# The scores of a graph layer computed only where the two triangles need them, and every engine's order written anew

## What is computed

```python
adj_tri = jnp.triu(adj, k=1)
diag_mask = jnp.triu(adj, k=0) - adj_tri
for l in range(L):
    m_left = jnp.einsum('bsh,oh->bso', h, W_left[l])
    m_right = jnp.einsum('bsh,oh->bso', h, W_right[l])
    u_left = jnp.einsum('bih,bjh->bij', h, m_left) / temper
    u_right = jnp.einsum('bih,bjh->bij', h, m_right) / temper
    u = u_left * adj_tri + u_left * diag_mask + u_right * jnp.swapaxes(adj_tri, 1, 2)
    delta_exp_u = jnp.exp(u) * adj
    attention = delta_exp_u / (jnp.sum(delta_exp_u, axis=2, keepdims=True) + 1e-10)
    h_lin = jnp.einsum('bsh,oh->bso', h, W_lin[l]) + b_lin[l]
    h = jax.nn.relu(_layer_norm(jnp.matmul(attention, h_lin), ln_a[l], ln_b[l]))
```

## Time and profile before

| | us |
|---|---|
| median of three runs (2846.2 to 2848.68) | 2846.78 |
| the profiled execution, device time | 2846.03 |
| its span, first to last instruction | 2844.2 |
| PE busy in it | 2792.3 (98%) |
| DVE busy | 2447.5 (86%) |
| ACT busy | 1784.8 (63%) |
| POOL busy | 1497.1 (53%) |
| mean granted TensorE clock | 0.992 |

### The profile page before, as it was taken

The page is one execution under the profiler, slowest core; times in us unless marked ns, Lnnn a source line. Parts: engine busy times, 40 slices in busy tenths (PEclk is TensorE's granted clock), DMA queues, the critical chain, the costliest instruction groups (busy, mean ns, idle before and its releaser), DMA issues.

```text
span 2844.2 us, 69230 instructions
## 1 busy us (share of the span) xinstructions
PE 2792.3 (98%) x24768; PEld 1793.3 (63%) x24768; DVE 2447.5 (86%) x8170; ACT 1784.8 (63%) x4107; POOL 1497.1 (53%) x1585
## 2 busy tenths in 40 slices
PE   7999999999999999999999999999999999999996
PEld 3566666666666666666666666666666666666654
DVE  4788988888888889888888888898888888888986
ACT  4556676656666556766566666567665667665664
POOL 2555565455554455654555654556545556445543
PEclk9999999999999999999999999999999999999998
DMA  4011011100111100111010111001111101110000
GB/s 163 20 35 43 21 43 43 46 32 24 43 43 43 46 32 21 46 40 46 32 35 32 43 43 46 32 21 46 40 46 32 46 21 43 43 46 32 21 28 21
DMA packets 55972, 112.18 MB, mean 39 GB/s; under 512 B 4944, under 2 KB 37712, under 8 KB 55632
## 3 DMA queue, kind: packets, MB, share of 16 engines
q1 hardware_dynamic: 55632, 107.76, 11.1%
HBM read 82.58 MB, written 25.17 MB: 38 GB/s over the span
## 4 chain that ended last, share of the span: by engine, by line
PE 97%; DVE 1%; issue 1%; ACT 1%; DMA 0%; POOL 0%; SPq 0%; POOLq 0%; DVEq 0%; ACTq 0%
PE psum L1243 70%; PE psum L1253 11%; PE psum L1304 9%; PE psum L1397 4%; PE psum L1371 3%; DMA xTin<-xT 0%; DMA s<-weights 0%; ACT w L587 0%; ACT w_hi L527 0%; DVE st L962 0%; POOL hl_lo L387 0%; DVE w_lo L785 0%; DVE st L908 0%; POOL e L416 0%; DVE y L900 0%
## 5 line engine op out<-in xcount | busy, mean ns | idle before, releaser
L587 ACT ACTIVATE w<-s,nmax 128x128 f32<-128x128 f32 x1536 | 474.1, 391 | 1.3 <-DVE nmax L837 1.2
L1243 PE MATMUL psum<-hT_hi,w_hi 128*128 128x512 f16 x1152 | 438.3, 381 | 13.5 <-POOL hT_lo L379 11.6
L1243 PE MATMUL psum<-hT_lo,w_hi 128*128 128x512 f16 x1152 | 438.0, 380 | 0.0
L1243 PE MATMUL psum<-hT_hi,w_lo 128*128 128x512 f16 x1152 | 437.9, 380 | 0.0
L527 ACT ACTIVATE nT_hi<-psum 128x512 f16<-128x512 f32 x384 | 228.3, 595 | 239.8 <-PE psum L1243 239.8
L461 POOL TENSOR_TENSOR fold<-s 128x768 f32<-128x768 f32 x128 | 232.7, 1818 | 224.5 <-DVE nmax L837 139.6
L837 DVE CUSTOM_DVE_ANT_0 s<-psum,adj 128x128 f32<-128x128 f32 x1536 | 343.1, 284 | 2.9 <-PE psum L1371 0.8
L527 ACT ACTIVATE hl_hi<-hl_raw 128x384 fp32r<-128x384 f32 x256 | 133.1, 520 | 300.5 <-DVE hl_raw L817 300.5
L387 POOL TENSOR_TENSOR hl_lo<-hl_raw,hl_hi 128x384 fp32r<-128x384 f32 x256 | 252.6, 993 | 125.7 <-ACT hl_hi L527 125.6
L527 ACT ACTIVATE pT_hi<-psum 128x512 f16<-128x512 f32 x384 | 224.0, 595 | 75.1 <-PE psum L1253 72.9
L804 DVE SCALAR_TENSOR_TENSOR nT_lo<-psum,nT_hi 128x512 f16<-128x512 f32 x384 | 253.5, 683 | 16.1 <-ACT nT_hi L527 16.1
(11 more groups left out here) (133 smaller groups left out, 8136.5 us busy)
## 6 DMA issues: line engine op xcount, KB each, us to landing
xTin<-xT SPq DMA_DIRECT2D x32, 768.0 KB, 4.6
xres<-x SPq DMA_DIRECT2D x32, 768.0 KB, 4.7
out<-y SPq DMA_DIRECT2D x128, 192.0 KB, 1.9
adjn<-adj SPq DMA_DIRECT2D x32, 256.0 KB, 4.9
adjT_sb<-adjT SPq DMA_DIRECT2D x32, 256.0 KB, 5.1
adj<-adj SPq DMA_DIRECT2D x32, 256.0 KB, 2.8
x<-weights SPq DMA_DIRECT2D x4, 576.0 KB, 5.8
s<-weights SPq DMA_DIRECT2D x3, 576.0 KB, 6.2
```

The lines of the kernel that those rows point to most:

```text
L587: last = nc.scalar.activation(w[:, m], s[b % 2][:, m], ACT.Exp, bias=nmax[b % 2][:, m:m + 1], scale=-1.0)
L1243: last = mm(dst, a, b, start=(i == 0), stop=(i == total - 1))
```

## The change

- Of the two 128 x 128 squares of a graph, only the part with j and i in the same half of the tokens is needed from both. The array's columns are taken as two tiles of 64 token rows. The first tile (rows 0 to 63) gets 192 moving columns: the right form of all 128 tokens and the left form of tokens 0 to 63. The second gets the right form of tokens 64 to 127 and the left form of all. So each matmul with 128 x 128 weights and 256 columns becomes two with 128 x 64 weights and 192 columns, into the upper and the lower 64 partitions of one bank. `nT` is laid out so that these 192 columns lie side by side.
- DVE multiplies 384 columns instead of 512 with the mask, and adds 128 instead of 256, in place in `uLR`.
- ACT takes the exponential in three instructions instead of one, each over 64 partitions, which put the parts at their places in `e`.
- POOL makes the mask in one instruction of 768 columns instead of two of 512, from an adjacency array that the host has cut to shape (`adjM`, 192 columns for a graph; it replaces the load of `adjn`). Five small instructions at the start prepare `keep`.
- The four lists and the bank table are written anew. On PE: `u(0,0)` and `u(0,1)` stand side by side; `th(2)` no longer stands between the parts of `scores(0)`; `nl(1,0)` stands before `pt(0,1)`; both `qk(0)` and `qk(1)` stand before the four `ctx(0)`; `u(1,0)` and others of the second half move by a step or two; `to(2)` stands before `hl(1,3)`.

```diff
 HCOL = FEAT + 2
+HALF = TOK // 2
+TRI = 3 * HALF
...
-        adjn = sb("adjn", [GROUP, TOK])
+        adjm = sb("adjm", [GROUP, TRI])
         adjT_sb = sb("adjT_sb", [2, GROUP, TOK])
-        mask = sb("mask", [GROUP, 2, TOK])
+        mask = sb("mask", [GROUP, TRI])
...
-        nT_hi, nT_lo = (sb(f"nT_{p}", [KB, 2, GROUP, TOK], f16) for p in ("hi", "lo"))
+        nT_hi, nT_lo = (sb(f"nT_{p}", [KB, GROUP, 2, TOK], f16) for p in ("hi", "lo"))
...
-        uLR = [sb(f"uLR{h}", [2, 2, TOK]) for h in range(2)]
+        uLR = [sb(f"uLR{h}", [2, TRI]) for h in range(2)]
...
-            [signal(f"{p}{l}", 2) for l in range(2)]
+            [signal(f"{p}{l}", 6 if p == "e_raw" else 2) for l in range(2)]
...
-                    sp.wait_ge(mask_ok.sem, mask_ok.upto(it, 2))
-                    sp.dma_start(adjn[:], adj[bass.ds(it + 1, 1)].rearrange("g i b j -> i (g b) j"))\
+                    sp.wait_ge(mask_ok.sem, mask_ok.upto(it, 1))
+                    sp.dma_start(adjm[:], adjM[bass.ds(it + 1, 1)].rearrange("g j b c -> j (g b) c"))\
...
+            for own in (slice(0, HALF), slice(HALF, TOK)):
+                nc.gpsimd.tensor_copy(keep[own, 0:HALF], keep_right[own, own]).then_inc(keep_ok, 1)
+                nc.gpsimd.tensor_copy(keep[own, TOK:TRI], keep_left[own, own]).then_inc(keep_ok, 1)
+            pool.wait_ge(keep_ok, 5)
...
                 pool.wait_ge(adj_in.sem, adj_in.upto(p.it + 1, 16))
-                pool.wait_ge(adjT_in.sem, p.upto(adjT_in, 16))
                 if p.l0:
                     pool.wait_ge(u_read[1].sem, p.upto(u_read[1], 2))
+                nc.gpsimd.tensor_tensor(mask[:], adjm[:], keep[:, None, :].to_broadcast([128, GROUP, TRI]), ALU.mult)\
+                    .then_inc(mask_ok.sem, 1)
...
-                pool.wait_ge(e_raw[l].sem, p.upto(e_raw[l], h + 1))
+                pool.wait_ge(e_raw[l].sem, p.upto(e_raw[l], 3 * (h + 1)))
+                if l == 0 and h == 0:
+                    pool.wait_ge(adjT_in.sem, adjT_in.upto(p.it, 16))
...
+                    two = slice(2 * h, 2 * h + 2)
+                    first, second = slice(0, HALF), slice(HALF, TOK)
+                    for j, i, src in ((slice(0, HALF), slice(0, TOK), slice(0, TOK)),
+                                      (second, second, first), (second, first, second)):
+                        nc.scalar.activation(e[j, two, i], uLR[h][j, :, src], ACT.Exp).then_inc(e_raw[l].sem, 1)
...
-                nc.vector.tensor_tensor(uLR[h][:], bank(f"u{l}", h).rearrange("p (b r t) -> p b r t", b=2, r=2),
+                    dve.wait_ge(mask_ok.sem, mask_ok.upto(p.it, 1))
+                nc.vector.tensor_tensor(uLR[h][:], bank(f"u{l}", h)[:, 0:2 * TRI].rearrange("p (b c) -> p b c", b=2),
                                         mask[:, 2 * h:2 * h + 2], ALU.mult).then_inc(u_read[l].sem, 1)
...
-                nc.vector.tensor_tensor(e[:, 2 * h:2 * h + 2], uLR[h][:, :, 0], uLR[h][:, :, 1], ALU.add)\
+                nc.vector.tensor_tensor(uLR[h][:, :, 0:HALF], uLR[h][:, :, 0:HALF], uLR[h][:, :, TOK:TRI], ALU.add)\
...
-                    dst = bank(f"u{l}", h)[:, g * 256:(g + 1) * 256].rearrange("p (r t) -> p r t", r=2)
-                    terms = [t for k in range(KB) for t in split(
-                        hT_hi[l][:, k, b], hT_lo[l][:, k, b], nT_hi[:, k, :, b], nT_lo[:, k, :, b])]
-                    for i, (a, m) in enumerate(terms):
-                        last = mm(dst, a, m, start=(i == 0), stop=(i == len(terms) - 1))
+                    dst = bank(f"u{l}", h)[:, g * TRI:(g + 1) * TRI]
+                    for n in range(3 * KB):
+                        k, t = divmod(n, 3)
+                        a = (hT_hi, hT_hi, hT_lo)[t][l][:, k, b]
+                        m = (nT_hi, nT_lo, nT_hi)[t][:, k, b].rearrange("p r t -> p (r t)")
+                        for j in range(2):
+                            own = slice(HALF * j, HALF * (j + 1))
+                            last = mm(dst[own], a[:, own], m[:, HALF * j:HALF * j + TRI],
+                                      start=(n == 0), stop=(n == 3 * KB - 1))
...
                 hl(p, 1, 0)
-                y2_power(p, 0)
                 folds(p, 3)
+                hl(p, 1, 1)
+                hl(p, 1, 2)
                 weigh(p, 1, 0)
-                hl(p, 1, 1)
+                weigh(p, 1, 1)
                 e_rest(p, 1, 0)
-                weigh(p, 1, 1)
-                hl(p, 1, 2)
                 e_rest(p, 1, 1)
                 hl(p, 1, 3)
+                mask_of(p)
                 y2_power(p, 1)
-                mask_left(p)
                 y2_power(p, 2)
-                mask_right(p)
...
                 x1_norm(p, 2)
                 x1_norm(p, 3)
+                hl(p, 0, 0)
                 hl(p, 0, 1)
+                exp_u(p, 0, 0)
                 x1t(p, 0)
-                exp_u(p, 0, 0)
                 x1t(p, 1)
+                x1t(p, 2)
                 exp_u(p, 0, 1)
-                x1t(p, 2)
                 round_e(p, 0, 0)
                 round_e(p, 0, 1)
+                hl(p, 0, 2)
+                hl(p, 0, 3)
...
+                to(p, 1)
                 exps(p, 3, 3)
-                to(p, 1)
+                fin(p, 0)
+                pt(p, 3, 0)
                 hl(p, 1, 1)
+                pt(p, 3, 1)
+                hl(p, 1, 2)
+                to(p, 2)
                 exp_u(p, 1, 0)
-                hl(p, 1, 2)
-                pt(p, 3, 0)
-                fin(p, 0)
+                exp_u(p, 1, 1)
                 round_e(p, 1, 0)
-                pt(p, 3, 1)
-                exp_u(p, 1, 1)
-                to(p, 2)
                 pt(p, 3, 2)
                 round_e(p, 1, 1)
...
                 y_variance(p)
-                u(p, 0, 0)
                 hl(p, 0, 0)
                 resid_inv(p)
+                setup(p, 4)
+                hl(p, 0, 1)
+                resid_norm(p, 0)
+                fin(p, 2)
+                resid_norm(p, 1)
+                u(p, 0, 0)
                 u_add(p, 0, 0)
-                resid_norm(p, 0)
-                resid_norm(p, 1)
-                hl(p, 0, 1)
                 u(p, 0, 1)
                 u_add(p, 0, 1)
+                hl(p, 0, 2)
                 x1t(p, 0)
                 x1t(p, 1)
                 x1t(p, 2)
...
                 nl(p, 0, 0)
+                nl(p, 0, 1)
                 pv(p, 3)
-                nl(p, 0, 1)
                 nl(p, 0, 2)
+                nl(p, 0, 3)
                 to(p, 3)
-                nl(p, 0, 3)
                 nl(p, 0, 4)
+                po(p, 3)
                 nl(p, 0, 5)
-                po(p, 3)
                 hl(p, 0, 0)
+                hl(p, 0, 1)
                 u(p, 0, 0)
-                hl(p, 0, 1)
                 u(p, 0, 1)
                 hl(p, 0, 2)
                 x1t(p, 0)
...
                 x1t(p, 2)
                 hl(p, 0, 3)
                 qk(p, 0)
+                qk(p, 1)
                 ctx(p, 0, 0)
                 ctx(p, 0, 1)
-                qk(p, 1)
                 ctx(p, 0, 2)
                 ctx(p, 0, 3)
                 qk(p, 2)
...
                 th(p, 0)
                 th(p, 1)
                 v(p, 0)
+                th(p, 2)
                 scores(p, 0, 0)
                 scores(p, 0, 1)
-                th(p, 2)
                 scores(p, 0, 2)
                 v(p, 1)
                 v(p, 2)
...
                 scores(p, 1, 1)
                 scores(p, 1, 2)
                 pt(p, 0, 0)
+                nl(p, 1, 0)
                 pt(p, 0, 1)
-                nl(p, 1, 0)
                 pt(p, 0, 2)
                 nl(p, 1, 1)
                 pv(p, 0)
...
                 nl(p, 1, 3)
                 pt(p, 1, 0)
                 pt(p, 1, 1)
+                nl(p, 1, 4)
                 pt(p, 1, 2)
-                nl(p, 1, 4)
                 po(p, 0)
                 nl(p, 1, 5)
+                pt(p, 2, 0)
                 pv(p, 1)
-                pt(p, 2, 0)
                 scores(p, 3, 0)
                 scores(p, 3, 1)
                 scores(p, 3, 2)
                 hl(p, 1, 0)
+                u(p, 1, 0)
                 pt(p, 2, 1)
-                u(p, 1, 0)
+                pt(p, 2, 2)
                 hl(p, 1, 1)
-                pt(p, 2, 2)
+                to(p, 1)
                 hl(p, 1, 2)
+                pv(p, 2)
                 pt(p, 3, 0)
-                to(p, 1)
                 pt(p, 3, 1)
-                pv(p, 2)
                 u(p, 1, 1)
                 pt(p, 3, 2)
+                to(p, 2)
                 hl(p, 1, 3)
-                to(p, 2)
                 po(p, 1)
                 po(p, 2)
                 ctx(p, 1, 0)
...
```

More of the change, by code:

```diff
@@ L28, in upto, with program @@
         return group * self.per_group + n
-def program(nc, x, xT, adj, adjT, weights, biases, ln_cols, ln_rows, out):
+def program(nc, x, xT, adj, adjT, adjM, weights, biases, ln_cols, ln_rows, out):
```

(36 more changed lines are left out.)

193 lines of the change are left out of this document (80 added, 113 removed).

## The result

| | before | after |
|---|---|---|
| median, us (four runs each) | 2846.75 (2846.20 to 2848.68) | 2803.10 (2801.84 to 2804.14) |
| the profiled execution, device time | 2846.03 | 2804.14 |
| its span | 2844.2 | 2802.3 |
| one pass | 86.63 | 85.23 |

The ratio is 0.9845, with a 95% interval of 0.9833 to 0.9857: 43.65 us less. The forecast was 2800.

A forecast was written before the change was run, and what follows sets the result against it. PE's moving columns were taken to bound every pass. From 2846.0 us: 61.7 less for u, 12.8 more for tiled blocks, 2 for waits gave 2799, put at 2800 for the median; range 2778 to 2840, chance 0.8.

The forecast's parts named there:

- PE's pitch: PE's u matmuls: a side-by-side pair of 192-column tiles takes 82.5 ns, making u 190.1 us instead of 251.8.
- Rival B: In u, the two column tiles run one after the other, 165 ns a pair: 2987 us; chance 0.04.
- rival A: In u, weight loads are no longer hidden: 112 ns a pair, 2865 us, or 142 ns and 2934; chance 0.10.
- The blocks: PE changing between whole array and tiles: 0.20 us a block, 96 added and 32 removed, 12.8 us more.
- The covers: Three places where other engines' results must reach PE in time; all were forecast to hold.
- (1): End of layer 1, hl_lo ready before ctx(1,3): slack shrinks from 1.2 to about 0.45 us, but holds.
- (2): DVE's norm ready before PE's x1t: slack shrinks from 1.05 to about 0.7 us.
- (3): DVE's third hT_lo ready for nl(1,0)'s seventh matmul: slack falls from 0.6 to about 0.1 to 0.2 us, the thinnest.
- The 2 us allowed there: Allowance over all passes for PE waiting for hT_lo at nl(1,0), added to the forecast sum.
- ends of the run 0: Not a follow-up run: start and end of the whole execution, for which the forecast sum has no term, 0.
- The other engines: DVE 1.1 us a pass less, ACT 2.4 more, POOL's mask about 1.8 to 1.9 us; worth nothing on PE.
- Rival C: A cover fails, likeliest nl(1,0) or x1t; PE waits 0.5 to 1.5 us a pass: 2815 to 2846 us; chance 0.13.

The follow-up runs named there:

- single-matmul run: Changed kernel with each pair of 192-column tile matmuls in u made one 128 x 128-weight matmul with the first tile's 192 columns: 2777.29 us, ratio 0.9758.
- the quarters: Changed kernel with u in four column tiles of 32 token rows and 160 columns: narrow layout 2770.44 us, ratio 0.9730; wide layout 2778.00 us, ratio 0.9757.
- the run with the wide forms: New orders and two column tiles, but the old kernel's bank shape, 512-column mask product, 256-column sum, one exponential, two masks: 2802.21 us, ratio 0.9841.
- the kernel with four tiles and the wide layout: New orders, u in four column tiles of 160 columns written into the old bank shape, with the old wide work behind PE: 2778.00 us, ratio 0.9757.

## Why the prediction was right, and where it was off

**PE's pitch.** The step that carried the forecast held to the nanosecond: 82.5 ns a pair, read off as 2.5 ns and 0.417 ns a column, and side by side as the row tiles of the earlier trace rows. The single-matmul run (1.49 for 18) and the quarters (69.2) show the same rule at two more places. Rival B, one tile after the other, is out in every `u` piece, and so is rival A, weight loads that show. The first loads of a `u` in the kernel after, as in the earlier trace rows:

```profile
1422.71 0.11 PEld L1306 LDWEIGHTS psum<-nT_hi,hT_hi 128*64 128x64 f16 x2 [0.32 <-issue]
1422.74 0.11 PEld L1306 LDWEIGHTS psum<-nT_lo,hT_hi 128*64 128x64 f16 x2
```

The second two begin 0.03 us behind the first two. Whether that is one load after another or two side by side, the run with the tiles one after the other tells, where only one tile's loads stand here:

```profile
1454.46 0.11 PEld L1306 LDWEIGHTS psum<-nT_hi,hT_hi 128*64 128x64 f16 x1 [0.32 <-issue]
1454.49 0.11 PEld L1306 LDWEIGHTS psum<-nT_lo,hT_hi 128*64 128x64 f16 x1
```

One load holds back the next of its tile for the same 0.03 us, against the 0.01 of a load of 128 columns in the earlier trace rows. That is the pace that the rival took; what it had wrong is the 0.06 for two, since the loads of a pair go side by side. None of it shows, since every pair has 82.5 ns of cover. The Trainium skill (TensorEngine Tiling (Array Packing), "Gotcha 2: Feature Incompatibilities") has fast weight load off in column tiles; that half the columns take longer (0.03 against 0.01 us) and not half as long agrees with it, and it costs nothing here.

**The blocks.** This is the term that was mis-sized. Forecast: 0.20 us each, net 0.40 a pass. Measured: 0.22 for layer 0's, 0.27 for each of layer 1's, 0.24 for the one removed, net 0.52. That is 0.12 us in 32 passes, 3.8 us. What was missed is mostly the part that isn't at the edge: a transpose right behind tiled work is late inside its own piece. (The rest is the first pair of a block, 0.02 to 0.03 us late.) It stood in the trace of before already: the earlier trace rows has eight transposes at 1.02 us, and those stand behind a `scores`. A piece of eight behind ordinary products, from the same chain, put beside it would have shown the 0.15:

```profile
1501.03 0.87 PE psum L1253 x8
```

The single-matmul run confirms the sum: 0.76 us for the three blocks, 0.12 x 3 + 0.15 x 2 + 0.10.

**The covers.** All three held with the sizes below, and PE waits at none of them. POOL and DVE in the kernel after, as in the earlier trace rows:

```profile
1437.53 0.86 POOL L385 TENSOR_TENSOR hl_lo<-hl_raw,hl_hi 128x384 fp32r<-128x384 f32 x1
```

```profile
1459.50 0.47 DVE L1056 TENSOR_SCALAR x<-x,yrstd,ynmr 128x384 f32<-128x384 f32 x1
...
1486.57 0.68 DVE L1029 TENSOR_TENSOR hT_lo<-h_raw,hT_hi 128x512 f16<-128x512 f32 x1
```

- (1) The last `hl_lo` ends at 1438.39, `ctx(1,3)` is due at 1433.00 + 27 x 0.1625 + 9 x 0.18 = 1439.0: 0.6 us to spare, 0.45 forecast.
- (2) The norm ends at 1459.97, `x1t` comes at 1461.55: 1.6 us, 0.7 forecast. Most of the difference is the norm itself: in the earlier trace rows its two instructions took 1.55 us together, the second of them 1.16 (last section), and here they take 0.47 each. The prediction had no reason for that; the cover was bigger by luck.
- (3) The third `hT_lo` ends at 1487.25, and PE, which starts `nl(1,0)` at 1487.19, needs it at its seventh matmul, 1488.5. That is 1.2 us where 0.1 to 0.2 was forecast, since the instruction takes 0.68 us and no longer 1.75. The 2 us allowed there were not needed. Here too the prediction did not foresee the shorter instruction.

Forecast against measured: -48.9 us for PE's work in 32 passes against -44.5 (32 x 1.39); +2 for waits against 0; ends of the run 0 against +2.6 (what 32 passes would save, less the 41.9 of the profiled execution). The sum is 5 us short in the profiled execution, 3 in the medians.

**The other engines.** Mask product 552 ns (546 forecast), the sum 347 (280), the added exponentials 0.3 us, the mask 1829 ns (1.8 to 1.9). ACT's pass is 57.5 us (57.7), DVE's 72.9 (75.0). DVE's further 2 us come from three forms that the change doesn't touch and the new orders made shorter: `hT_lo` (99.5 to 66.4 us in the run), `rs` L869 (53.1 to 26.9) and the norm L1057 (48.8 to 29.7), 2.4 us a pass, of which the sum, slower than forecast, takes 0.3 back. One group by form, after:

```profile
L593 ACT ACTIVATE e<-uLR 64x128 f32<-64x128 f32 x256 | 64.5, 298 | 3.1
```

That they are worth nothing was right for this change, by the run with the wide forms. But the reason held only with the new orders: under the old ones the same exponentials make PE late, and the whole gain is gone.

**Rival C**, a failed cover, was the right one to watch. The change avoids it; the runs with the old orders and with both layer-1 scores together are that rival, and its price range (2815 to 2846) was too low at its upper end: 2850 in one, 2867 in the other.

## What to carry to other kernels

Where a product needs only part of its columns for part of its rows, column tiles cost their widest tile's moving columns and nothing for their number (here two of 192 and four of 160), if they are issued in turn; each block of them costs 0.22 us, and 0.05 more ahead of transposes, so gather them, but not at the cost of the cover they give to others. A saving on the bounding engine and the order of all engines are one change: here the first alone gave nothing (+3 us), the second alone -9, both -44. Price a change of mode by comparing equal pieces of the chain with and without it ahead, not by the edge alone.

## What was not expected of the hardware

**DVE and POOL stand in each other's way.** In the earlier trace rows the third `hT_lo` took 1.75 us, and 0.68 after. POOL's timeline of the kernel before at that time:

```profile
1509.13 1.82 POOL L461 TENSOR_TENSOR fold<-s 128x768 f32<-128x768 f32 x1
```

The fold ran to 1510.95 and `hT_lo`, which starts at 1509.75, ended 0.55 us behind that: it seems to have waited for all of the fold. It is so in every pass: of the 96 `hT_lo` of the kernel before, 31 start while a fold runs and take 1.75 to 1.83 us, all ending 0.55 us behind it, and the other 65 take 0.69. In the kernel with four tiles and the wide layout, DVE's sum of two halves took 1.17 us at 1445.39 (0.42 is its usual time), ending 0.29 us behind the first of these two POOL instructions, which takes 1.00 us:

```profile
1445.27 2.00 POOL L387 TENSOR_TENSOR hl_lo<-hl_raw,hl_hi 128x384 fp32r<-128x384 f32 x2 [2.03 <-ACT hl_hi L527]
```

The norm of cover (2) is a third place. In the kernel before its first instruction there takes 0.47 us and the second, shown with POOL's instruction of that time, 1.16:

```profile
1482.23 1.16 DVE L1057 TENSOR_SCALAR x<-x,yrstd,ynmr 128x384 f32<-128x384 f32 x1
...
1482.02 1.15 POOL L387 TENSOR_TENSOR hl_lo<-hl_raw,hl_hi 128x384 fp32r<-128x384 f32 x1 [0.63 <-ACT hl_hi L527]
```

Of its 64 norms, 31 start beside this `hl_lo` and take 1.16 us, and 33 take 0.47; in the kernel after none starts beside a POOL instruction and all take 0.47. The 31 end 0.22 us behind the `hl_lo`, less than their own length, so they are not held for all of it. Over the run the group of `hT_lo` shows the effect, before and after:

```profile
L1030 DVE TENSOR_TENSOR hT_lo<-h_raw,hT_hi 128x512 f16<-128x512 f32 x96 | 99.5, 1037 | 27.1 <-ACT hT_hi L630 27.1
```

```profile
L1029 DVE TENSOR_TENSOR hT_lo<-h_raw,hT_hi 128x512 f16<-128x512 f32 x96 | 66.4, 691 | 21.6 <-ACT hT_hi L629 21.6
```

The form is the same and its mean fell from 1037 to 691 ns. With the old scores under the new orders it is 691 too, and with the new scores under the old orders 1035: it comes with the orders alone. These orders free `hT_lo` from the fold, and put the sum partly beside a POOL instruction instead. The Trainium skill (SBUF — State Buffer, "🔬 SBUF: two separate sides") says that GpSimd and a VectorE instruction with two SBUF inputs take a shared port in turn, each for its whole instruction; the first two places above and the group agree. The norm reads one tensor and two columns of scalars, and no run shows whether the rule covers that form. The rule was not weighed in the prediction, where cover (3) took the 1.75 us for the cost of the work itself. That this is the cause is argued from when the instructions run, though without an exception among the 96 `hT_lo` of the kernel before; no run took the POOL instruction away.

**A tile runs ahead of program order**: it begins with three matmuls of the other tile still to start, as the run with the tiles one after the other shows (25 pitches instead of 18 or 36).

**A transpose behind tiled work is late twice**: 0.10 us for the change, and 0.05 more before the piece is over (1.02 against 0.87 for eight).
